# Layer 1's attention: the next keys are turned and copied ahead of the outputs instead of behind them

## What is computed

```python
Q = (x @ Wq + bq).reshape(Bsz, Tlen, H, dh)
K = (x @ Wk + bk).reshape(Bsz, Tlen, H, dh)
V = (x @ Wv + bv).reshape(Bsz, Tlen, H, dh)
Qp = jax.nn.relu(Q)
Kp = jax.nn.relu(K)
Qc, Qs = (Qp * cosw, Qp * sinw)
Kc, Ks = (Kp * cosw, Kp * sinw)
...
S_cos = S_cos + kc[..., :, None] * v[..., None, :]
S_sin = S_sin + ks_[..., :, None] * v[..., None, :]
...
num = jnp.einsum('bhi,bhij->bhj', qc, S_cos) + jnp.einsum('bhi,bhij->bhj', qs, S_sin)
den = jnp.sum(qc * z_cos + qs * z_sin, axis=-1)
...
return out @ Wo + bo
```

## Time and profile before

| | |
|---|---|
| median of 3 runs | 982.62 us (980.2 to 985.75) |
| the profiled execution | 973.3 us, its span 972.0 us |
| TensorE busy | 853.4 us, 88% of the span |
| VectorE busy | 639.1 us, 66% |
| ScalarE busy | 436.6 us, 45% |
| GpSimd busy | 388.8 us, 40% |
| granted TensorE clock, mean | 0.953 of full speed |

### The profile page before, as it was taken

How to read it: one execution, slowest core, us unless ns; L and a number is a source line. 1 busy time by engine, 2 the same in 40 slices (tenths; PEclk the granted TensorE clock), 3 DMA queues, 4 the chain that set the end, 5 groups by cost and what they waited for, 6 DMA issues and landing times.

```text
span 972.0 us, 33029 instructions
## 1 busy us (share of the span) xinstructions
PE 853.4 (88%) x13726; PEld 717.8 (74%) x13726; DVE 639.1 (66%) x1719; ACT 436.6 (45%) x940; POOL 388.8 (40%) x399
## 2 busy tenths in 40 slices
PE   6899963599990899999899989999999988899998
PEld 5577753498980588888778778788887776777676
DVE  7778773356543366665776857888868777556754
ACT  5465433144431655555454454564644443332321
POOL 5247777043336444555336344456423333100000
PEclk9999985699995799999999999999999999899999
DMA  9601104533302000000100001000000000000000
GB/s 304 185 10 39 36 20 163 165 117 105 90 28 76 1 25 4 25 3 8 41 3 25 3 3 46 3 3 6 4 2 4 3 3 4 3 12 12 22 23 22
DMA packets 47890, 40.12 MB, mean 41 GB/s; under 512 B 3553, under 2 KB 42736, under 8 KB 47360
## 3 DMA queue, kind: packets, MB, share of 16 engines
q1 hardware_dynamic: 44272, 32.84, 11.1%
q0 software_dynamic: 3328, 5.16, 1.6%
q10 hardware_dynamic: 144, 0.02, 0.0%
HBM read 23.90 MB, written 15.84 MB: 41 GB/s over the span
## 4 chain that ended last, share of the span: by engine, by line
PE 71%; DVE 14%; issue 7%; POOL 3%; ACT 2%; DMA 2%; ACTq 0%; SPq 0%; POOLq 0%; DVEq 0%
PE psum L1290 9%; PE psum L1415 7%; PE psum L1388 6%; PE psum L1364 6%; PE psum L1318 5%; PE psum L1853 4%; PE psum L1344 4%; PE psum L1081 4%; PE psum L1092 4%; PE psum L1886 4%; PE psum L1330 3%; PE psum L1300 3%; PE psum L1403 3%; POOL disp L274 2%; PE psum L413 1%
## 5 line engine op out<-in xcount | busy, mean ns | idle before, releaser
L1775 POOL TENSOR_TENSOR sb_a_qr<-sb_h,sb_a_csq 128x512 f32<-128x512 f32 x64 | 80.5, 1278 | 127.1 <-PE psum L1364 127.1
L1775 POOL TENSOR_TENSOR sb_a_qr<-sb_a_qp,sb_a_csq 128x512 f32<-128x512 f32 (+1 forms) x64 | 71.6, 1141 | 135.9 <-PE psum L1364 135.9
L1290 PE MATMUL psum<-sb_wkv,sb_a_hs 128*128 128x512 f32 x384 | 122.9, 428 | 1.7 <-DVE sb_a_va L1652 0.9
L1522 ACT ACTIVATE sb_a_vr<-sb_a_va,sb_consts 128x520 f32<-128x520 f32 x128 | 86.5, 726 | 3.8 <-DVE sb_a_va L1652 3.2
L1364 PE MATMUL psum<-sb_a_mid,sb_a_qr 64*64 64x65 f32 x2048 | 73.5, 220 | 5.2 <-issue 5.2
L1053 POOL DMA_INDIRECT chosen<-sb_m_h3t,sb_e_row x40 | 41.3, 1032 | 88.0 <-ACTq L1138 78.3
L1388 PE MATMUL psum<-sb_a_vr,sb_a_kb 64*64 64x130 f32 x1920 | 73.3, 280 | 0.8 <-issue 0.8
L274 POOL DMA_INDIRECT disp<-sb_h,sb_slot x64 | 64.9, 1014 | 21.3 <-issue 17.4
L1290 PEld LDWEIGHTS psum<-sb_wkv,sb_a_hs 128*128 128x128 f32 x384 | 63.1, 191 | 13.3 <-issue 2.0
L1415 PE MATMUL psum<-sb_a_wo,sb_a_ot 128*128 128x128 f32 x512 | 68.3, 287 | 4.1 <-issue 4.0
L1364 PEld LDWEIGHTS psum<-sb_a_mid,sb_a_qr 64*64 64x64 f32 x2048 | 67.3, 136 | 5.8 <-issue 5.8
(11 more groups left out here) (260 smaller groups left out, 1996.2 us busy)
## 6 DMA issues: line engine op xcount, KB each, us to landing
sb_e_w<-in_w SPq DMA_DIRECT2D x24, 256.0 KB, 3.2
chosen<-sb_empty SPq DMA_DIRECT2D x8, 512.0 KB, 6.5
sb_a_g<-chosen SPq DMA_DIRECT2D x14, 256.0 KB, 3.6
disp<-sb_empty SPq DMA_DIRECT2D x4, 650.0 KB, 9.6
sb_e_x<-disp SPq DMA_DIRECT2D x8, 325.0 KB, 5.2
sb_a_wo<-in_wo SPq DMA_DIRECT2D x4, 512.0 KB, 7.4
out<-sb_x SPq DMA_DIRECT2D x7, 256.0 KB, 2.3
sb_x<-in_x SPq DMA_DIRECT2D x3, 512.0 KB, 7.8
```

What stands on the lines that cost most here:

```text
L1290: ins = pe.matmul(self.bank[0], hs[:, part, at:at + P], self.Wkv[ws][:, h, w], start=(k == 0), stop=(k == 2))
L1522: ins = act.activation(self.Vr[i % 2][:, :, k, :], self.Va[i % 3][:], ACT.Copy, scale=self.c[("cos1", "sin1")[k]][:, n:n + 1])
L1775: ins = g.tensor_tensor(self.Qr[i % 2][:, k, :, t], qp, rows(self.csQ[:, k, c * P + t.start:(c + 1) * P], PH), ALU.mult)
```

## The change

In each step of the loop `keys_turned1(i + 1)` goes ahead of `outputs_turned(i - 1)` on TensorE, and `keys_scalar(i + 1)` ahead of `outputs_scalar(i - 1)` on ScalarE. No instruction and no wait is added or taken away, and the other engines' programs stay the same.

```diff
--- before.py
+++ after.py
@@ -1455,10 +1455,10 @@
                 self.keys_tensor(i + 2, 0)
             if 0 <= i and i // 8 + 1 < NGRP:
                 self.queries_block(i // 8 + 1, i % 8, 2, i + 8, i)
+            if known(i + 1):
+                self.keys_turned1(i + 1, xadd, h1, h3, lg)
             if known(i - 1):
                 self.outputs_turned(i - 1)
-            if known(i + 1):
-                self.keys_turned1(i + 1, xadd, h1, h3, lg)
             if known(i + 2):
                 self.keys_tensor(i + 2, 1)
             if known(i):
@@ -1565,10 +1565,10 @@
                 self.values_rotated(i + 1)
             if 0 <= i and i // 8 + 1 < NGRP:
                 self.queries_scalar(i // 8 + 1, i % 8, 2)
+            if known(i + 1):
+                self.keys_scalar(i + 1)
             if known(i - 1):
                 self.outputs_scalar(i - 1)
-            if known(i + 1):
-                self.keys_scalar(i + 1)
             if known(i + 2):
                 self.keys_cut(i + 2)
             if i == -1 or (known(i) and i % 8 == 5 and i // 8 + 2 < NGRP):
```

## The result

The changed kernel is slower: 1006.91 us median (1003.24 to 1007.88) against 981.84 us of the kernel before (980.2 to 985.75), a ratio of 1.0243, 95% interval 1.0201 to 1.0284. The forecast was 1000.4 us, +17.8, within 991 to 1009.

A forecast was written before the change was run, and what follows sets the result against it. TensorE was taken to bound the kernel (71% of the chain), ScalarE's copies having little slack before the scores. +21.0 - 0.6 - 1.2 - 1.4 = +17.8 us on the median 982.62 gives 1000.4, range 991 to 1009.

The forecast's parts named there:

- TensorE has nothing to win in a usual step: TensorE's outputs' turn in 50 usual steps: hardly any wait to fill, sum 0; all waits there 10.8 us.
- The scores come 0.42 us later in 50 steps: Scores wait for output copies queued behind the keys' copy on ScalarE: 50 x 0.42 = +21.0 us.
- The swap on TensorE costs nothing: Keys' and outputs' transposes both take 0.44 us, so values start at the same time: 0.
- -0.6 in five steps, -1.2 in six: Steps whose output copies waited for transposes: two win 0.2 us, three 0.07; six late steps 0.2 each.
- -1.4 for stalls that swallow the delay: TensorE's "issue" stalls behind the scores keep their own time and absorb 0 to 1.7 us; -1.4 taken.
- The difference between the profiled execution and the median: Profiled execution 973.3 us, 9.3 below the median 982.62; no step depends on it, so sum added to median.
- Rival (a): Faster: keys' turn fills TensorE's wait before the outputs' turn, copies not missed; all 10.8 us, 971.8; chance 0.04.
- the 0.07 us of slack: Before the scores in a usual step: the output copies can end about 0.07 us later unnoticed.
- (b): Delay swallowed by later "issue" waits and VectorE's late chains in about 25 steps: +7.3, 989.9; chance 0.07.
- (c): TensorE's clock falls more often near the new pauses; ten more slow stretches add 17 us, 1017; chance 0.07.

The follow-up runs named there:

- the three ratios: The full change against the kernel before, measured three times: 1.0243, then 1.0194 on chip 4 and 1.0215 on chip 6.
- the kernel with the keys last: Kernel before with TensorE's order alone made queries, outputs turned, values, keys turned, scores: 1.0145 (1.01 to 1.0191).
- the unchanged kernel's second profile: Kernel before, unchanged, run again against itself on chip 6: 1.0001 (0.9976 to 1.0026).

## Why the prediction was right, step by step

The direction, the place and the mechanism were right, and the time lay in the range; the size was forecast at 17.8 us and measured at 24, 19 and 21 us by the three ratios.

- *TensorE has nothing to win in a usual step.* Right. Its wait for the outputs fell from 10.8 to 6.0 us, 4.8 in all, in the few steps named, and these steps grew shorter by less than that.
- *The scores come 0.42 us later in 50 steps.* Right as to the scores: 1.88 against 1.46 us behind the queries' copy, and 0.79 of pause. The step itself grew by 0.42 to 0.45: the first 16 steps, which stalls and clock falls hardly touch, took 123.33 us and not 116.17, 0.45 each. A part of the few hundredths more lies behind the scores: the masked scores on VectorE start 0.78 and not 0.76 us behind them, and the state's update 1.59 and not 1.57. The term is 50 x 7.16 / 16 = 22.4 and not 21.0.
- *The swap on TensorE costs nothing.* Right in the full change, where the outputs' transposes were ready at 586.18 + 0.75 = 586.93 and ScalarE came to them at 587.12. The cover is thin, 0.19 us: alone, this half costs 0.25 us a step. The forecast also had the keys' transposes ready 0.69 us after their first load. Where they stand right behind a stream of 512 columns it is 0.86 (389.79 to 390.65 in the kernel with the keys last), so in the changed kernel they were ready at about 585.63 + 0.86 = 586.49, still ahead of ScalarE at 586.64.
- *-0.6 in five steps, -1.2 in six.* Right as to the long waits: 0.20 us from the outputs' turn to the scores in all eight. The short ones gave 0.01 to 0.06 where they could be read, and I had 0.07.
- *-1.4 for stalls that swallow the delay.* This is the step that failed. Some of the stalls right behind the scores did vanish (L1364 stood seven times before and four times after), but the remaining ones grew, L1364's sum from 6.5 to 8.0 us, and those of L1403 and L1415 from 9.6 to 10.7. In three profiles of the changed kernel the three together are 16 to 19 us, in two of the kernel before 16. The net is nothing to +4, not -1.4. The traces also say what TensorE probably waited for. In the loop of each of these five profiles 19 or 20 stalls of "issue" are longer than 0.45 us, the pauses ahead of the scores left out. Each ends 1.2 to 1.6 us after a packet of the DMA queue that brings instructions (q8), while only 5 or 6% of all weight loads start in that distance; 92 such packets of 16 KB land in the loop, one for about 123 loads. So TensorE was most likely out of instructions there. No run tests it, and the forecast treated these stalls as waits that keep their own time.
- With the measured terms: +22.4 - 1.7 = 20.7, and with 0 to 4 for the stalls 21 to 25. The loops were 17.7 to 24.5 us longer than the 502.4 of the unchanged kernel's second profile. What is left between profiles is stalls and clock falls, of either sign.
- *The difference between the profiled execution and the median* was left as it stood, and rightly: most of it lies in what stands ahead of the attention, which differs by chip.

Rival (a), faster, died on the 0.07 us of slack. Of (b) there is a trace, as told. For (c) there is none.

## What to carry to other kernels

Two pairs of swaps look like one edit, but each queue that they stand in has its own next customer. Before a block is moved ahead of another, ask on every engine that takes part: who waits for the one that is moved back, and how much slack does it have? Here the moved copy had no hurry for microseconds and the copies behind it had 0.07 us.

A gain on an engine's idle time is bounded by the waits that the trace shows for that very block; here 10.8 us. The wait shrank by 4.8 and the steps by some 1.7 in all. The bound is read in a minute and says whether the rest of the analysis is about a gain or about a loss.

When a cost is taken away in an experiment, the time comes back only down to the next bound. Work out that second bound first, or a shorter copy that gives back 0.19 of 0.45 us looks like a refutation.

## What was not expected of the hardware

Transposes that stand behind other transposes on TensorE were ready for a copy 0.74 to 0.75 us after their first load; a block that stood alone, 0.69 to 0.70; right behind a stream of 512 columns, 0.86 to 0.87 (62 steps of the kernel with the keys last). A wait for the output copies reached TensorE's scores 0.11 to 0.12 us after the copy's end wherever it was the last one.

The pause ahead of the 64*64 matmuls was 0.36 us behind the 512-column values and 0.17 behind the 128-column transposes, and the work between stretched by as much. So the pause goes with the stream that ends, and moving a short block into it gained nothing here. The Trainium skill, TensorEngine Tiling (Array Packing), section Key Properties, says that a change of the tiling mode drains TensorE, and gives no length. The trace agrees in that a pause stands at this change, 0.36 or 0.37 us in 62 of 64 steps of the kernel before and 0.17 us in 61 with the keys last. That the change of tile is its cause was not tested by a run.
